# Expert gate and up products in three fp32r parts instead of fp32, with 47 slots and a ring of 7

## The reference

```python
x = x + attn(layernorm(x))       # 16 heads of 8, no softmax: (q k^T / n**sigmoid(m)) v, q and k normalised, out @ Wo + bo
h = layernorm(x)
# routing: top 1 of 16 experts by h @ router_w.T, score = sigmoid(top logit)
routed_in = hidden[None] * scores.T[:, :, None]
gate, up = split(einsum('nth,nhf->ntf', routed_in, gate_up_proj))          # 128 -> 2 x 128
expert_sum = einsum('ntf,nfh->nth', up * silu(gate), down_proj).sum(0)     # 128 -> 128
shared = silu(h @ shared_gate_w.T) * (h @ shared_up_w.T) @ shared_down_w.T # 128 -> 512 -> 128
x = x + shared + expert_sum
```

## Time and profile before

| | |
|---|---|
| time, median of 3 runs | 212.82 us (212.21 to 212.95) |
| the profiled execution's own time | 212.76 us |
| its span, first to last instruction | 209.9 us |
| TensorE busy | 190.5 us (91%) |
| VectorE busy | 143.8 us (69%) |
| ACT busy | 103.2 us (49%) |
| GpSimd busy | 113.8 us (54%) |
| granted TensorE clock | 1.00 throughout |

### The profile page before, as it was taken

The page is one execution under the profiler, slowest core; times in us unless marked ns, Lnnn a source line. Parts: engine busy times, 40 slices in busy tenths (PEclk is TensorE's granted clock), DMA queues, the critical chain, the costliest instruction groups (busy, mean ns, idle before and its releaser), DMA issues.

```text
span 209.9 us, 3828 instructions
## 1 busy us (share of the span) xinstructions
PE 190.5 (91%) x1126; PEld 155.2 (74%) x1126; DVE 143.8 (69%) x500; ACT 103.2 (49%) x234; POOL 113.8 (54%) x142
## 2 busy tenths in 40 slices
PE   0696699999989999999988989999999999999994
PEld 0242566666767787788677979899999988988883
DVE  4679999999999958776545767946635325236555
ACT  3423365893657798852514556556653332232230
POOL 6002504647898885767540077757777778760000
PEclk9999999999999999999999999999999999999999
DMA  5999993000100101111135455621111110028425
GB/s 164 295 391 283 173 404 145 5 0 25 40 30 25 38 25 41 52 38 53 39 76 114 105 126 144 159 60 40 41 45 40 45 48 0 0 55 282 167 96 204
DMA packets 17751, 21.59 MB, mean 103 GB/s; under 512 B 3240, under 2 KB 11951, under 8 KB 17476
## 3 DMA queue, kind: packets, MB, share of 16 engines
q1 hardware_dynamic: 14016, 15.87, 26.5%
q0 software_dynamic: 2560, 4.24, 6.3%
q10 hardware_dynamic: 1156, 1.26, 1.8%
HBM read 13.95 MB, written 8.44 MB: 107 GB/s over the span
## 4 chain that ended last, share of the span: by engine, by line
PE 43%; DVE 15%; POOL 14%; DMA 13%; issue 9%; SPq 5%; ACT 0%; ACTq 0%; DVEq 0%; POOLq 0%
DMA x_slots<-h_rows,pos 9%; PE bank L1242 8%; POOL x_slots L353 8%; PE quad_banks L1279 7%; PE quad_banks L1220 5%; PE quad_banks L1222 5%; PE quad_banks L1221 5%; SPq L252 4%; DVE qkv L771 4%; PE bank L1298 4%; POOL qkv L322 4%; DVE st L733 3%; DMA w_qkv<-w_in 3%; PE bank L1287 2%; DVE ss L779 2%
## 5 line engine op out<-in xcount | busy, mean ns | idle before, releaser
L362 POOL DMA_INDIRECT y_back<-yg,xg x48 | 47.2, 984 | 29.1 <-ACT yg L555 13.6
L851 DVE TENSOR_TENSOR s_act<-quad_banks,sg_act 128x512 f32<-128x512 f32 x32 | 22.0, 688 | 26.4 <-PE bank L1242 12.6
L527 ACT ACTIVATE sg_act<-quad_banks 128x512 f32<-128x512 f32 x32 | 19.2, 598 | 42.5 <-PE quad_banks L1222 42.4
L353 POOL DMA_INDIRECT x_slots<-h_rows,pos x32 | 31.4, 980 | 12.5 <-issue 6.9
L322 POOL TENSOR_TENSOR qkv<-qkv,rn 128x512 f32<-128x512 f32 x16 | 17.0, 1078 | 26.9 <-DVE rn L784 26.7
L1242 PEld LDWEIGHTS bank<-sdT,s_act 128*128 128x128 f32 x224 | 28.0, 191 | 1.5
L1242 PE MATMUL bank<-sdT,s_act 128*128 128x128 f32 x224 | 28.9, 275 | 0.0
L1135 PE MATMUL quad_banks<-w_c,xT 128*128 128x384 f32 x64 | 24.8, 520 | 2.1 <-DVE qkv L771 1.3
L1279 PE MATMUL quad_banks<-w_gu,xgT 128*128 x96 | 22.9, 382 | 0.8 <-ACT xgT L538 0.8
L1135 PEld LDWEIGHTS quad_banks<-w_c,xT 128*128 128x128 f32 x64 | 11.9, 203 | 10.8 <-issue 3.7
L1279 PEld LDWEIGHTS quad_banks<-w_gu,xgT 128*128 128x128 f32 x96 | 17.3, 190 | 2.9 <-issue 1.0
(11 more groups left out here) (146 smaller groups left out, 370.0 us busy)
## 6 DMA issues: line engine op xcount, KB each, us to landing
xg<-x_slots SPq DMA_DIRECT2D x48, 65.0 KB, 1.9
xT<-x_t SPq DMA_DIRECT2D x8, 256.0 KB, 7.0
xres<-L_attn_x SPq DMA_DIRECT2D x8, 256.0 KB, 7.1
w_gu<-gate_up SPq DMA_DIRECT2D x1, 2048.0 KB, 13.7
h_rows<-y_back SPq DMA_DIRECT2D x8, 256.0 KB, 4.8
x_slots<-zeros SPq DMA_DIRECT2D x1, 1040.0 KB, 15.7
w_dn<-down SPq DMA_DIRECT2D x1, 1024.0 KB, 15.6
out<-xres SPq DMA_DIRECT2D x4, 256.0 KB, 2.3
```

The lines of the kernel that those rows point to most:

```text
L353: g.indirect_dma_start(out=x_slots, out_offset=bass.IndirectOffsetOnAxis(ap=pos[:, t:t + 1], axis=0), in_=h_rows[:, t, :], in_offset=None) ...
L362: nc.gpsimd.indirect_dma_start(out=y_back, out_offset=bass.IndirectOffsetOnAxis(ap=xg[:, n, D + 1:D + 2].bitcast(I32), axis=0), in_=yg[:, ...
L851: v.tensor_tensor(s_act[:, n % 2], pair[:, 2 * (n % 2) + 1], sg_act[:, n % 2], ALU.mult).then_inc(s_act_rdy, 1)
```

## The change

The gate and up product of the experts is split like the shared ones. The weights `w_gu` become a high part (`w_guh`, rounded to fp32r by ACT, `expert_hi`, four pieces of four experts) and a low part (the rest, left in `w_gu` by VectorE, `expert_lo`, four pieces). The turned rows get a high part (ACT, `rows_copy`, as before but into fp32r) and a low part (VectorE, the new `rows_lo`, one per group, from PSUM). `gT_sb`, for which the product and the next `turn_rows` wait, is now counted up by `rows_lo`. TensorE does three fp32r matmuls of 256 columns for each slot. The last group has 3 slots (`own(g)`). The ring `yg` has 7 places: `take_y(g)` from group 7 on waits until the sends of group g - 7 are done. `zeros` is one row per partition, read for all 16 regions. The order of what was there before stays on all engines; the new entries are put between.

```diff
-    SLOTS = NG * Q
+    SLOTS = NT + E - 1
-    YRING = 12
+    YRING = 7
+    EC = E // 4
-        w_gu = sb("w_gu", [P, E, F2])
+        w_gu = sb("w_gu", [P, E, F2], F32R)
+        w_guh = sb("w_guh", [P, E, F2], F32R)
-            zeros = sb_a("zeros", [P, E, W])
+            zeros = sb_a("zeros", [P, W])
-        xgT = sb("xgT", [P, 2, Q * P])
+        xgT = sb("xgT", [P, 2, 2, Q * P], F32R)
+        def own(g):
+            return range(min(Q, SLOTS - g * Q))
-            sp.dma_start(heads_of[0:P], zeros[:]).then_inc(zero_st, 16)
+            sp.dma_start(heads_of[0:P], zeros[:].unsqueeze(1).broadcast_to([P, E, W])).then_inc(zero_st, 16)
-            g.iota(zeros[:, :, D + 1].bitcast(I32), pattern=[[P, E]], base=T, channel_multiplier=1).then_inc(z_done, 1)
+            g.iota(zeros[:, D + 1:D + 2].bitcast(I32), pattern=[[0, 1]], base=T, channel_multiplier=0).then_inc(z_done, 1)
...
+            def expert_hi(n):
+                if n == 0:
+                    act.wait_ge(ld_wg, 16)
+                part = slice(EC * n, EC * n + EC)
+                a.copy(w_guh[:, part], w_gu[:, part].bitcast(F32)).then_inc(e_hi, 1)
             def rows_copy(g):
...
-                a.copy(xgT[:, g % 2], ps_gT[:]).then_inc(gT_sb, 1)
+                here = slice(0, P * len(own(g)))
+                a.copy(xgT[:, g % 2, 0, here], ps_gT[:, here]).then_inc(gT_hi, 1)
...
             silu_shared(3)
+            expert_hi(0)
             silu_shared(4)
             hT_hi(5)
+            expert_hi(1)
             silu_shared(5)
+            expert_hi(2)
...
             silu_shared(8)
+            expert_hi(3)
             silu_shared(9)
...
+            def expert_lo(n):
+                dve.wait_ge(e_hi, n + 1)
+                part = slice(EC * n, EC * n + EC)
+                v.tensor_tensor(w_gu[:, part], w_gu[:, part].bitcast(F32), w_guh[:, part].bitcast(F32), ALU.subtract
+                                ).then_inc(e_lo, 1)
+            def rows_lo(g):
+                dve.wait_ge(gT_hi, g + 1)
+                if g >= 2:
+                    dve.wait_ge(e_gu_mm, g - 1)
+                here = slice(0, P * len(own(g)))
+                v.tensor_tensor(xgT[:, g % 2, 1, here], ps_gT[:, here], xgT[:, g % 2, 0, here].bitcast(F32), ALU.subtract
+                                ).then_inc(gT_sb, 1)
...
             act_shared(5)
+            expert_lo(0)
             slot_rows()
             act_shared(6)
+            expert_lo(1)
             take_table()
+            expert_lo(2)
             act_shared(7)
             add_shared(0)
+            expert_lo(3)
             act_shared(8)
             add_shared(1)
             score_logit(0)
+            rows_lo(0)
             score(0)
             score_logit(1)
             act_shared(9)
+            rows_lo(1)
             gated(0)
             score_logit(2)
             turned_act(0)
+            rows_lo(2)
             score(1)
             score_logit(3)
             gated(1)
             score(2)
             score_logit(4)
+            rows_lo(3)
             turned_act(1)
             score_logit(5)
             score(3)
             score(4)
             gated(2)
+            rows_lo(4)
             score_logit(6)
             turned_act(2)
             gated(3)
+            rows_lo(5)
             score_logit(7)
...
             score_logit(11)
             gated(7)
+            rows_lo(9)
             turned_act(7)
+            rows_lo(10)
             gated(8)
             gated(9)
+            rows_lo(11)
             score(10)
             turned_act(8)
...
                 if g == 0:
                     pe.wait_ge(table_rdy, 1)
-                    pe.wait_ge(ld_wg, 16)
+                    pe.wait_ge(e_lo, E // EC)
...
-                    mm = te.matmul(gate_up_banks(g % 2)[:, j, :], xgT[:, g % 2, P * j:P * j + P],
-                                   gu_cols[:, bass.ds(held[g][j] * 2, F2)], start=True, stop=True)
+                    to = gate_up_banks(g % 2)[:, j, :]
+                    hi, lo = xgT[:, g % 2, 0, P * j:P * j + P], xgT[:, g % 2, 1, P * j:P * j + P]
+                    te.matmul(to, hi, gu_cols[0][:, bass.ds(held[g][j] * 2, F2)], start=True, stop=False)
+                    te.matmul(to, hi, gu_cols[1][:, bass.ds(held[g][j] * 2, F2)], start=False, stop=False)
+                    mm = te.matmul(to, lo, gu_cols[0][:, bass.ds(held[g][j] * 2, F2)], start=False, stop=True)
```

More of the change, by code:

```diff
@@ L220, in rank_of @@
             return log_bank(c)[:, 320:320 + Q]
+        def own(g):
+            return range(min(Q, SLOTS - g * Q))
         def slot_values(which, g, engine, top):
             _, vals = nc.values_load_multi_w_load_instructions(
-                table_cols[0:1, which * SLOTS + g * Q:which * SLOTS + g * Q + Q], engines=(engine,), min_val=0,
+                table_cols[0:1, which * SLOTS + g * Q:which * SLOTS + g * Q + len(own(g))], engines=(engine,), min_val=0,
                 max_val=top, skip_runtime_bounds_check_because="VectorE made them of counts and ranks in range")
@@ L250, in load @@
                         sp.wait_ge(landed, 16 * NT // 2)
-                for j in range(Q):
+                for j in own(g):
                     sp.dma_start(xg[:, g * Q + j, :], x_slots[bass.ds(first[j], P), :]).then_inc(xg_ld[g], 16)
@@ L554, in take_y @@
                         act.wait_ge(landed, 16 * len(range(turn, Q * (g - YRING + 1), 3)))
-                a.copy(yg[:, g % YRING], ps_yg[:].rearrange("p (j d) -> p j d", d=D)).then_inc(yg_rdy, 1)
+                n = len(own(g))
+                a.copy(yg[:, g % YRING, 0:n], ps_yg[:, 0:P * n].rearrange("p (j d) -> p j d", d=D)).then_inc(yg_rdy, 1)
             std_x(0)
@@ L877, in score_logit @@
             def score_logit(g):
-                dve.wait_ge(xg_ld[g], 16 * Q)
-                here = slice(g * Q, g * Q + Q)
+                dve.wait_ge(xg_ld[g], 16 * len(own(g)))
+                here = slice(g * Q, g * Q + len(own(g)))
                 link(v.tensor_tensor(logit_inv[:, here], xg[:, here, D], xg[:, here, D], ALU.mult))
@@ L905, in turned_act @@
                     dve.wait_ge(e_dn_mm, g - 1)
-                v.tensor_copy(e_actT[:, g % 2], ps_aT[:]).then_inc(aT_sb, 1)
+                here = slice(0, P * len(own(g)))
+                v.tensor_copy(e_actT[:, g % 2, here], ps_aT[:, here]).then_inc(aT_sb, 1)
             def scale_mask():
@@ L1049, in _ @@
             gated(4)
+            rows_lo(6)
             score_logit(8)
@@ L1052, in _ @@
             gated(5)
+            rows_lo(7)
             turned_act(4)
@@ L1061, in _ @@
             gated(6)
+            rows_lo(8)
             score(9)
@@ L1264, in turn_rows @@
             def turn_rows(g, after=None):
-                pe.wait_ge(xg_ld[g], 16 * Q)
+                pe.wait_ge(xg_ld[g], 16 * len(own(g)))
                 free(after)
-                for j in range(Q):
+                for j in own(g):
                     mm = te.transpose(ps_gT[:, P * j:P * j + P], xg[:, g * Q + j, 0:D], ident[:])
```

7 lines of the change are left out of this document (4 added, 3 removed).

## The result

The changed kernel takes 218.71 us (median of 6 runs, 217.77 to 220.59), the kernel before on the same chip 212.88: ratio 1.0315 [1.0272, 1.0358]. Slower was forecast, but 215.6, with 217.4 as the upper end: the loss is about twice the one worked out. The profiled execution took 220.14 with a span of 218.3. (Medians are over all executions; a ratio compares only those in the faster of two states that the executions show, so the two can differ by some tenths of a per cent.)

A forecast was written before the change was run, and what follows sets the result against it. TensorE was taken as the bound from 126 us, GpSimd almost as critical. Late start 2.3 plus waits 6.4, less 0.99, 3.5 and 0.8, made 3.4 (3.1 as laid out); the end 2.8 late: 212.76 + 2.8 = 215.6, range 213.4 to 217.4.

The forecast's parts named there:

- the second low part of the weights: VectorE subtraction priced at 1.2, fitting in the 2.08 wait for the turned table; table moves from 104.49 to 105.63.
- stretch a: From VectorE's first operation behind s_act(5) to the cast of the table; forecast 6.68.
- b: Stretch from the cast of the table to the first product of group 0; forecast 7.87.
- c: Stretch from the first product of group 0 to the span's end; forecast 99.2.
- The products: Gate and up on TensorE: 0.12 a product, 1.44 a group, 0.29 saved per group, 3.5 over twelve.
- the dearer product: Rival, gate and up on TensorE: 0.16 a product, 1.92 a group, giving 218.5; chance 0.10.
- exposed loads: Rival, gate and up on TensorE: weight loads of 0.19 not hidden, 0.93 a slot, giving 237; chance 0.02.
- The waits: Expert stage: waits of 6.4 in sum as TensorE, ACT and VectorE take turns in each group.
- The ring and the row of zeros: Ring of 7 before take_y and one row of zeros for clearing: both put at nothing.
- slot 48: Dropping the 48th slot saves 0.8 on TensorE and one send of 1.29 on GpSimd.
- The saving arrives: Rival: VectorE's new work falls into its waits, GpSimd decides near 186, 211.5; chance 0.08 including in-between results.
- The late start alone: Rival: expert-stage waits half as long as laid out, only the late start remains, 213.5 to 214.2; chance 0.18.

The follow-up runs named there:

- e3_both: Changed kernel with slot-table stride 48 and GpSimd's low parts of h (chunks 3, 4) waiting for the weights' four low parts: 216.11 us, ratio 1.0159.
- e2_pool: Changed kernel with only GpSimd's low parts of h for chunks 3 and 4 waiting for the weights' four low parts: 217.82 us, ratio 1.0225.
- e1_align: Changed kernel with only the slot table's stride changed from 47 to 48: 217.56 us, ratio 1.0236.
- e7_small: Kernel before with 47 slots (table stride 48), ring of 7 and one row of zeros; gate and up stay fp32: ratio 0.9933.
- e9_no_lo: e4_waits without low parts of rows and weights and without GpSimd's wait; products reuse high parts, so the block is not computed: ratio 0.9887.
- e4_waits: e3_both with VectorE's low parts of the weights moved into its waits, first rows' low part ahead of the logits: 214.75 us, ratio 1.0151.
- e11_no_rows_lo: e4_waits without the low parts of the rows; the third product reuses the high rows, so the block is not computed: ratio 0.9972.
- e5_balance: e4_waits with the copy of the turned act (turned_act) moved from VectorE to ACT: 214.07 us, ratio 1.0061.
- e8_shift: Kernel before with only TensorE's half of the slot table moved by three elements: 213.99 us, ratio 1.0041.
- e10_shift2: Kernel before with SyncE's half of the slot table one element off a multiple of 16 bytes, TensorE's two off; one run, no ratio.

## Why the prediction was wrong

The direction and the mechanism held: a late start and VectorE's new work on the round of each group eat more than the products save. The size did not, and two steps of about equal weight failed: one term of the sum, the second low part of the weights, was three times as long as priced, and one, the load of slot values, was put at nothing by not being named. Without both, e3_both has a ratio of 1.0159 [1.0088, 1.0229] (after 1.0315 [1.0272, 1.0358]); the forecast, 215.6 to 212.76, is 1.0133. In the profiled execution the span ends 5.6 later than the forecast's 212.7: 1.5 in stretch a, 1.6 in b, 2.9 in c, less 0.3 for an earlier beginning of a.

**The first step that failed: "the second fits in the 2.08 that VectorE waits for the turned table; the table moves from 104.49 to 105.63".** The price of 1.2 was taken from a reduction, which reads one SBUF operand. One of its eight, in the profile of before, ran beside GpSimd (42.37 to 43.58, GpSimd's subtraction from 42.38 to 43.65) and took 1.21 all the same. The new subtraction reads two. GpSimd's low parts of h read two as well; the two that follow the last scatter fell into this wait, and the subtraction took 3.69. In e2_pool and e3_both, where they come later, it takes 1.2 and the table stands where it was forecast. The Trainium skill, "SBUF — State Buffer", section "SBUF: two separate sides", says that VectorE and GpSimd share a pair of ports under an exclusive lock, which an operation of VectorE with two SBUF inputs needs against a GpSimd operation that reads SBUF, and that the loser is blocked outright; the trace agrees, with 2.49 of excess beside 2.53 of GpSimd (2.50 in before, so GpSimd was not held up). The Trainium skill also gives the pair, there, to whichever starts first; the trace differs, as VectorE's row begins at 103.16, 0.06 before GpSimd's, and VectorE lost. I had not asked what runs beside the new operation. In the profile of before, GpSimd's two stand at 104.74 to 107.24, 0.25 behind the end of that wait, so its row there would have shown them as neighbours and not as an overlap.

**The clock, a term that was missing.** Forecast: b = 113.5 - 105.63 = 7.87. e1_align and e3_both measure 7.83. After has 9.42: TensorE was busy 2.48 of the 5 us from 104 to 109, and from 110 to 113 the granted clock was 0.50; the down groups at 110.66 took until 113.74 with 16 products, 3.1 instead of the 1.8 of before (107.97 to 109.75). The idle time alone does not explain it: e1_align has the same 2.48 of the 5 us from 104 to 109, and its clock stays at 1.00. The fall is not part of every execution: of the six runs the three with a mean granted clock of 1.000 took 217.77 to 218.29, the three with 0.977 to 0.992 took 219.14 to 220.59. The former lie above the 217.4 of the range too, so the forecast would have failed without it.

**The second step that failed: the load of slot values, put at nothing by not being named.** The 47 in the table's stride moved TensorE's loads off a multiple of 16 bytes. After a wait of TensorE it is exposed, 3.0 in the profile of after, though part of that only takes the place of other waits. In the kernel before it costs 0.4% by itself; in the changed one the ratios give 0.8% (after and e1_align) and 0.7% (e2_pool and e3_both), both with intervals that overlap.

**The products: right pace, too much saving.** They follow each other by 0.117 (0.12 taken), so the dearer product and the exposed loads are refuted. But the first of a group takes 0.22 (127.07 to 127.29), so a group is 1.51 and not 1.44, and it saves 0.22 instead of 0.29. All in all less still: c without TensorE's waits in it is 97.0 - 0.4 = 96.6 in e7_small and 97.2 - 2.5 = 94.7 in e9_no_lo, so 1.9 where twelve times 0.29, 3.5, had been put into the sum. In e1_align, whose low parts are made, it is 100.2 - 4.5 = 95.7: of the 1.9, 0.9 is left.

**The waits: too many.** 6.4 outside group 0 were laid out, e1_align shows 4.5. These two errors partly cancel, which is luck: for c the forecast was 212.7 - 113.5 = 99.2, and e1_align, with fast loads at the full clock, measures 100.2. (The chances do not add up either: by the rivals' shares slower has 0.62 + 0.09 + 0.12 = 0.83, not 0.78.)

**Right.** The high parts of the weights (1.04 each) hide on ACT. rows_lo is 0.69, and TensorE waits for it. GpSimd is no longer waited for near 187, though both it and TensorE get there later than forecast. The ring and the row of zeros cost nothing that can be seen, and slot 48 is worth what was worked out, within e7_small's interval.

**The rivals.** "The saving arrives" is what e9_no_lo shows once VectorE is free: GpSimd is waited for near 186, as it said, and a small gain is left (1.1% [0.6, 1.6] with slot 48). "The late start alone" is refuted: in e4_waits, with the table back in time, 1.5% of loss remained, and e11_no_rows_lo takes it away. So the low parts of the rows, an added link between ACT's copy and TensorE's product in every group, are the main price of the change as e4_waits has it. How much of it is the link and how much the work on VectorE is not separated: e5_balance keeps the link, takes another operation off VectorE and gets back 0.9%, about half.

**Open.** Why the granted clock falls in some executions and not in others (five of the twelve runs of e5_balance show a mean below 0.995), and what a fall costs by itself: no run here prices it alone. Where the rest of the products' saving goes, 1.9 instead of twelve times 0.22, and 0.9 where the low parts are made, was not found in single rows.

## What to carry to other kernels

Before an operation with two SBUF operands is put into VectorE's idle time, look at GpSimd's row in the same microseconds and next to them: the idle time is only free if GpSimd is not at work on SBUF there, and GpSimd's own work can be held up by VectorE's (the scatters of e4_waits). When a count changes, follow it into every stride that a register load or a table lookup depends on. Splitting a product into cheap ones is paid for by who makes the parts: here TensorE won 1 to 2 us at most, and each group's round got one more step on an engine that was already next to full.

## What the runs showed of the hardware

A load of four values from SBUF into an engine's registers takes 0.33 on TensorE and 0.30 on SyncE when they begin at a multiple of 16 bytes from the start of the table. It takes 1.00 on TensorE when they begin two or three elements of 4 bytes off it, and 0.87 on SyncE one element off (e8_shift, e10_shift2). Three values took 0.78 on TensorE three elements off the multiple (after), but also 0.775 on it, and 0.675 on SyncE (e1_align, last group): so it is the four values on the multiple that are fast. Elsewhere it is 0.22 to 0.26 for each value, as if they were fetched one by one. The Trainium skill, "Runtime: NRT & Kernel Launch", section "Instruction fetch mechanics", gives some 200 ns a register for this instruction, which it knows as a load from HBM; this table lies in SBUF, and the traces come near that figure everywhere but in the four values on the multiple.

A VectorE operation with one PSUM and one SBUF operand was not stretched beside GpSimd: in the kernel before, s_act took 0.69 while GpSimd subtracted from 104.74 to 107.24.

```profile
105.65 0.69 DVE L851 TENSOR_TENSOR s_act<-quad_banks,sg_act 128x512 f32<-128x512 f32 x1 [0.91 <-PE bank L1242]
```
```profile
104.74 2.50 POOL L332 TENSOR_TENSOR hT<-hT_full,hT 128x512 fp32r<-128x512 f32 x2
```

GpSimd's scatters were stretched from 0.96 to 1.68, 1.72 and 2.01 where they began behind a VectorE subtraction of two SBUF operands (e11_no_rows_lo, e4_waits); each ended 0.84 after it.
